# Edge counts by 90 groups of 14 destinations in pairs, in place of 60 windows of 21

## What is computed

```python
def rgat_conv(x, W, q, k, b, src, dst, etype, heads, out_ch, n_nodes):
    xr = jnp.einsum('nd,rdf->rnf', x, W)
    oi = xr[etype, dst]
    oj = xr[etype, src]
    qi = oi @ q
    kj = oj @ k
    alpha = jax.nn.leaky_relu(qi + kj, NEG_SLOPE)
    m = jax.ops.segment_max(alpha, dst, num_segments=n_nodes)
    e = jnp.exp(alpha - m[dst])
    z = jax.ops.segment_sum(e, dst, num_segments=n_nodes)
    a = e / (z[dst] + EPS)
    msg = (a[:, :, None] * oj.reshape(-1, heads, out_ch)).reshape(-1, heads * out_ch)
    out = jax.ops.segment_sum(msg, dst, num_segments=n_nodes)
    return out + b
```

## Time and profile before

| | |
|---|---|
| median of 3 runs | 1680.54 us (1675.92 to 1681.16) |
| profiled execution, first to last instruction | 1668.4 us |
| PE busy | 1571.1 us, 94% of the span |
| DVE busy | 1312.2 us, 79% |
| ACT busy | 808.3 us, 48% |
| POOL busy | 144.7 us, 9% |
| TensorE's clock, mean granted | 0.984 of full speed |

### The profile page before, as it was taken

The page is one execution under the profiler, slowest core; times in us unless marked ns, Lnnn a source line. Parts: engine busy times, 40 slices in busy tenths (PEclk is TensorE's granted clock), DMA queues, the critical chain, the costliest instruction groups (busy, mean ns, idle before and its releaser), DMA issues.

```text
span 1668.4 us, 34838 instructions
## 1 busy us (share of the span) xinstructions
PE 1571.1 (94%) x10783; PEld 1138.5 (68%) x10784; DVE 1312.2 (79%) x2631; ACT 808.3 (48%) x1072; POOL 144.7 (9%) x280
## 2 busy tenths in 40 slices
PE   5899988988999999999999999989999999999987
PEld 3566666766556666699999999976555555555544
DVE  8699869989479999288898998972774477777785
ACT  6331115552235654388888888962222233333342
POOL 3000010000100000000000000000000133333340
PEclk9999999999999999999999999989999999999999
DMA  6111125420456663540132133023765521101212
GB/s 208 37 60 62 62 59 171 156 81 29 134 183 219 200 200 120 175 136 31 62 94 62 31 116 118 12 92 93 211 202 190 191 96 56 37 20 56 76 51 93
DMA packets 129296, 178.56 MB, mean 107 GB/s; under 512 B 15510, under 2 KB 100607, under 8 KB 129203
## 3 DMA queue, kind: packets, MB, share of 16 engines
q1 hardware_dynamic: 129202, 177.38, 33.8%
HBM read 120.47 MB, written 56.88 MB: 106 GB/s over the span
## 4 chain that ended last, share of the span: by engine, by line
PE 70%; issue 16%; DVE 7%; ACT 2%; DMA 2%; DVEq 1%; POOL 1%; SPq 0%; POOLq 0%; ACTq 0%
PE ps L2210 23%; PE ps L2164 14%; PE ps L2270 7%; PE ps L2269 7%; PE ps L1983 5%; PE ps L2075 3%; PE ps L1970 2%; PE ps L1971 2%; PE ps L1972 2%; DVE oh_q L1466 1%; PE ps L2281 1%; PE ps L2147 1%; DVE oh_p L1467 1%; PE ps L2026 1%; DVE stat L1435 1%
## 5 line engine op out<-in xcount | busy, mean ns | idle before, releaser
L2210 PE MATMUL ps<-xrh,pf 128*128 (+1 forms) x2400 | 397.3, 328 | 4.8 <-DVE pf L1748 4.8
L2210 PEld LDWEIGHTS ps<-xrh,pf 128*128 128x128 f32 x2400 | 390.8, 190 | 11.2 <-issue 8.8
L2269 PE MATMUL ps<-x,ph 128*128 (+1 forms) x600 | 195.3, 325 | 12.1 <-POOL pl L989 12.0
L1970 PE MATMUL ps<-w_hi,xt_hi 128*128 128x384 f16 x600 | 196.9, 328 | 10.0 <-DVE ev L1794 3.2
L1748 DVE SCALAR_TENSOR_TENSOR pf<-vb,CT 128x1260 f32<-128x1260 f32 x118 | 172.8, 1467 | 32.5 <-PE ps L2210 32.5
L1971 PE MATMUL ps<-w_lo,xt_hi 128*128 128x384 f16 x600 | 196.9, 328 | 0.0
L2270 PE MATMUL ps<-x,ph 128*128 (+1 forms) x600 | 196.7, 328 | 0.0
L1972 PE MATMUL ps<-w_hi,xt_lo 128*128 128x384 f16 x600 | 196.6, 328 | 0.0
L1466 DVE TENSOR_SCALAR oh_q<-pat,codeT,neg_w 125x630 f16<-125x630 uint16 x420 | 185.2, 441 | 13.1 <-PE ps L1983 7.2
L1744 DVE SCALAR_TENSOR_TENSOR vb<-vb,tb 128x1260 f32<-128x1260 f32 x118 | 169.9, 1466 | 12.6 <-ACT vb L1220 11.7
L1656 DVE CUSTOM_DVE_ANT_0 tt_junk<-kbc,mb 126x1260 bf16<-126x1260 f32 x120 | 169.1, 1465 | 11.7 <-issue 11.7
(11 more groups left out here) (264 smaller groups left out, 2400.4 us busy)
## 6 DMA issues: line engine op xcount, KB each, us to landing
qbc<-tq_d SPq DMA_DIRECT2D x12, 1260.0 KB, 6.3
wst<-in_L_gnn_W SPq DMA_DIRECT2D x60, 192.0 KB, 3.2
xr_d<-ev SPq DMA_DIRECT2D x60, 192.0 KB, 2.0
x_d<-ev SPq DMA_DIRECT2D x60, 192.0 KB, 2.3
mb_d<-mb SPq DMA_DIRECT2D x30, 310.1 KB
mb<-mb_d SPq DMA_DIRECT2D x30, 310.1 KB
xrh<-xr_d SPq DMA_DIRECT2D x3, 2880.0 KB, 15.5
x<-x_d SPq DMA_DIRECT2D x2, 3840.0 KB, 18.3
```

The costliest lines, as they stand in the source:

```text
L1970: pe.matmul(ps[:, bank, 0:CW], a_hi, hi[:, k, :], start=(k == 0), stop=False)
L2210: mm = pe.matmul(out[b], pf[j][:, b * DB:b * DB + P], x, start=(first and b % 2 == 0), stop=False, skip_group_check=True)
L2269: pe.matmul(ps[:, bank, 0:CW], p, cols(off, off + CW), start=start, stop=False, skip_group_check=True)
```

## The change

- A window becomes a group of 14 destinations (WN = 14), 90 groups, which are worked on in 45 pairs. A tile of a group is `oh_q` of 420 columns and one matmul of 420 columns into one bank; the pair's two groups go to two neighbouring banks. ScalarE's copy and SyncE's store take a pair at a time (2 x 420 columns, 45 instead of 60).
- Each group has three fixed tiles (TF = 3) and a loop of single tiles, for which `oh_q` and `oh_p` have four rotating places (TR = 4) with semaphores counted tile by tile; place and tile are found in registers. From the edge lists of this input: 39 groups take one step of the loop and 51 take two, so 411 tiles, 9.13 for a pair (91 in W_K, 183 in W_V, 28 in W_S, 109 in W_Q).
- Each group has two table words (first tile with count; running total). PE and DVE thus read four words for each pair, where they read one for each window.
- The codes and slots of the fixed tiles are laid out ahead by POOL (`cw`, `sw`: a loop of 90 steps, each with one table read, an addition and a copy of 125 x 3), and VectorE waits for `cw_done`. The fixed `oh_q` is then made with one operand from memory instead of two.
- The pairs lie: 10 in W_K, 20 in W_V, 3 in W_S and 12 in W_Q (two for each query block, ahead of its fourth step and at its end). None lies in the attention. At the start of a query block PE reads eight words instead of three.
- CT comes back in units of three groups, `sel` and the selections for it are laid out for three groups (12 selections on POOL instead of 8), and three small operations on the table become one.

The diff, cut to its core:

```diff
-WN = 21
+WN = 14
 NWN = ND // WN
 KN = WN * R
 QN = NB * KN
-QH = QN // 2
-NTAB = 64
+NTAB = 96
...
-CT_EARLY = 14
-TF = 4
-TM = 3
-TG = TF + TM
+CT_EARLY = 7
+TF = 3
+TR = 4
+TG = 2 * TF + TR
 NTP = NT + 8
-MAXG = -(-(NT - TF) // TM)
+MAXG = NT - TF
+WU = WD // WN
+NWP = NWN // 2
...
+        cb = [place(f"cb{j}", [P, 2 * QN], U16, 185344 + 1696 * j) for j in range(2)]
+        cc_ = [place(f"cc{j}", [P, 2 * QN], U16, 141312 + 1696 * j) for j in range(2)]
+        cw = place("cw", [P, NWN * TF], F32, 173056)
+        sw = place("sw", [P, NWN * TF], F32, 174144)
+        tabrow = place("tabrow", [1, 2 * NTAB], I32, 175232)
...
-        def window(eng, w):
-
-            word = eng.value_load(tabrow[0:1, ds(w, 1)], min_val=0, max_val=(NWN * MAXG << 16) + (MAXG << 9) + NT)
+        def window(eng, s):
+
+            word = eng.value_load(tabrow[0:1, ds(2 * s, 1)], min_val=0, max_val=(MAXG << 9) + NT)
+            first = eng.value_load(tabrow[0:1, ds(2 * s + 1, 1)], min_val=0, max_val=NWN * MAXG)
             tile0 = eng.snap(word & 511, min_val=0, max_val=NT - 1)
-            count = eng.snap((word >> 9) & 127, min_val=1, max_val=MAXG)
-            first = eng.snap(word >> 16, min_val=0, max_val=NWN * MAXG)
+            count = eng.snap(word >> 9, min_val=1, max_val=MAXG)
             return tile0, count, first
 
+        def windows(eng, w):
+
+            return [window(eng, 2 * w + u) for u in range(2)]
+
         W_K, W_V, W_S, W_Q = 0, NB, 3 * NB, 3 * NB + 3
-        QW = 3
-        W_A = W_Q + QW * K6
-
-        def block_windows(i):
-
-            return range(W_A + i, min(W_A + i + 1, NWN))
-
-        assert W_A + NB >= NWN and WT_TILES == K6 * K6
+        QW = 2
+        assert W_Q + QW * K6 == NWP and WT_TILES == K6 * K6
...
-            sp.dma_start(ct_d[:, ds(w, 1), :].rearrange("p o n -> p (o n)"), stage[u][:, :]).then_inc(ct_out[u], 16)
+            sp.dma_start(ct_d[:, ds(2 * w, 2), :].rearrange("p o n -> p (o n)"), stage[u][:, :]).then_inc(ct_out[u], 16)
...
-            for i in range(NB):
-                for w in block_windows(i):
-                    store_window(sp, w, cc_, (w - W_Q) % 2)
...
-            pool.wait_ge(e_row, 7)
+            pool.wait_ge(tab_io, 32)
+            with pool.Fori(0, NWN) as s:
+                word = pool.value_load(tabrow[0:1, ds(2 * s, 1)], min_val=0, max_val=(MAXG << 9) + NT)
+                tf = nc.s_assert_within(pool.snap(word & 511, min_val=0, max_val=NT - 1), 0, NT - 1,
+                                        skip_runtime_bounds_check_because="the table holds first tiles of 0 to NT - 1")
+                pool.tensor_tensor(cw[0:ET, ds(TF * s, TF)], codeT[0:ET, ds(tf, TF)], neg_w[0:ET, ds(s, 1)].to_broadcast([ET, TF]), ALU.add)
+                pool.tensor_copy(sw[0:ET, ds(TF * s, TF)], sloT[0:ET, ds(tf, TF)]).then_inc(cw_done, 1)
...
-                act.activation(stage[u][:, :].rearrange("p (q n) -> p q n", q=2), ps[:, bank:bank + 2, 0:QH], ACT.Copy).then_inc(ct_ev, 1)
+                act.activation(stage[u][:, :].rearrange("p (q n) -> p q n", q=2), ps[:, bank:bank + 2, 0:QN], ACT.Copy).then_inc(ct_ev, 1)
...
-            for i in range(3):
+            for i in range(2):
                 dve.sem_inc(oh_free[i], 1)
-
-            def one_hot(u, codes, slots, k, w):
-
-                dve.tensor_scalar(oh_q[0:ET, u, :], pat[0:ET, :], codes[:, k:k + 1], neg_w[0:ET, ds(w, 1)], ALU.subtract, ALU.is_equal)
-                return dve.tensor_scalar(oh_p[0:ET, u, :], iota_l[0:ET, :], slots[:, k:k + 1], None, ALU.is_equal)
-
-            def one_hots(w, tile0, count, first):
-                tf = nc.s_assert_within(tile0, 0, NT - 1, skip_runtime_bounds_check_because="the table holds first tiles of 0 to NT - 1")
-                codes, slots = codeT[0:ET, ds(tf, TF)], sloT[0:ET, ds(tf, TF)]
-                for i in range(2):
-                    dve.wait_ge(oh_free[i], w + 1)
-                    for u in range(2 * i, 2 * i + 2):
-                        last = one_hot(u, codes, slots, u, w)
-                    last.then_inc(oh_rdy[i], 1)
-                with dve.Fori(0, count) as jj:
-                    n1 = dve.snap(first + jj + 1)
-                    t0 = dve.snap(nc.s_assert_within(tf + TM * jj + TF, TF, NTP - TM, skip_runtime_bounds_check_because="tile0 + TF + TM * count <= NTP for every window of the table"))
-                    more, more_slots = codeT[0:ET, ds(t0, TM)], sloT[0:ET, ds(t0, TM)]
-                    dve.wait_ge(oh_free[2], n1)
-                    for u in range(TM):
-                        last = one_hot(TF + u, more, more_slots, u, w)
-                    last.then_inc(oh_rdy[2], 1)
+            dve.sem_inc(oh_free[2], TR)
+
+            def one_hots(w, of_w):
+
+                for u in range(2):
+                    tile0, count, first = of_w[u]
+                    s = 2 * w + u
+                    dve.wait_ge(cw_done, s + 1)
+                    dve.wait_ge(oh_free[u], w + 1)
+                    for t in range(TF):
+                        dve.tensor_scalar(oh_q[0:ET, TF * u + t, :], pat[0:ET, :], cw[0:ET, ds(TF * s + t, 1)], None, ALU.is_equal)
+                        last = dve.tensor_scalar(oh_p[0:ET, TF * u + t, :], iota_l[0:ET, :], sw[0:ET, ds(TF * s + t, 1)], None, ALU.is_equal)
+                    last.then_inc(oh_rdy[u], 1)
+                    with dve.Fori(0, count) as jj:
+                        n1 = dve.snap(first + jj + 1)
+                        t0 = dve.snap(nc.s_assert_within(tile0 + jj + TF, TF, NTP - 1, skip_runtime_bounds_check_because="tile0 + TF + count <= NTP for every window of the table"))
+                        o = dve.snap((n1 & (TR - 1)) + 2 * TF, min_val=2 * TF, max_val=TG - 1)
+                        dve.wait_ge(oh_free[2], n1)
+                        dve.tensor_scalar(oh_q[0:ET, ds(o, 1), :].rearrange("p o n -> p (o n)"), pat[0:ET, :], codeT[0:ET, ds(t0, 1)],
+                                          neg_w[0:ET, ds(s, 1)], ALU.subtract, ALU.is_equal)
+                        dve.tensor_scalar(oh_p[0:ET, ds(o, 1), :].rearrange("p o n -> p (o n)"), iota_l[0:ET, :], sloT[0:ET, ds(t0, 1)],
+                                          None, ALU.is_equal).then_inc(oh_rdy[2], 1)
...
-                        of_w = window(dve, W_K + 2 * ii + j + 1)
+                        of_w = windows(dve, W_K + 2 * ii + j + 1)
                         k_sum(1, NB + 2 * ii + j, j)
-                        one_hots(W_K + 2 * ii + j + 1, *of_w)
+                        one_hots(W_K + 2 * ii + j + 1, of_w)
...
-                    if k in (1, 3, 4)[:QW - 1]:
-                        count_part(wa + (1, 3, 4).index(k) + 1)
+                    if k == 2:
+                        count_part(wa + 1)
...
-                count_part(wa + QW)
+                if more:
+                    count_part(wa + QW)
...
-                for w in block_windows(i):
-                    if w + 1 < NWN:
-                        count_part(w + 1)
...
-            def count_window(w, bank, count, first):
+            def count_windows(w, bank, of_w):
 
                 pe.wait_ge(ct_ev, w + 1)
-
-                def tile(u, start):
-                    for q in range(2):
-                        last = pe.matmul(ps[:, bank + q, 0:QH], oh_p[0:ET, u, :], oh_q[0:ET, u, q * QH:(q + 1) * QH],
-                                         start=start, stop=False, skip_group_check=True)
-                    return last
-
-                for i in range(2):
-                    pe.wait_ge(oh_rdy[i], w + 1)
-                    for u in range(2 * i, 2 * i + 2):
-                        last = tile(u, u == 0)
-                    last.then_inc(oh_free[i], 1)
-                with pe.Fori(0, count) as jj:
-                    n1 = pe.snap(first + jj + 1)
-                    pe.wait_ge(oh_rdy[2], n1)
-                    for u in range(TF, TG):
-                        last = tile(u, False)
-                    last.then_inc(oh_free[2], 1)
+                for u in range(2):
+                    _, count, first = of_w[u]
+                    pe.wait_ge(oh_rdy[u], w + 1)
+                    for t in range(TF):
+                        last = pe.matmul(ps[:, bank + u, 0:QN], oh_p[0:ET, TF * u + t, :], oh_q[0:ET, TF * u + t, :],
+                                         start=(t == 0), stop=False, skip_group_check=True)
+                    last.then_inc(oh_free[u], 1)
+                    with pe.Fori(0, count) as jj:
+                        n1 = pe.snap(first + jj + 1)
+                        o = pe.snap((n1 & (TR - 1)) + 2 * TF, min_val=2 * TF, max_val=TG - 1)
+                        pe.wait_ge(oh_rdy[2], n1)
+                        pe.matmul(ps[:, bank + u, 0:QN], oh_p[0:ET, ds(o, 1), :].rearrange("p o n -> p (o n)"),
+                                  oh_q[0:ET, ds(o, 1), :].rearrange("p o n -> p (o n)"),
+                                  start=False, stop=False, skip_group_check=True).then_inc(oh_free[2], 1)
...
```

(25 more changed lines are left out.)

101 lines of the change are left out of this document (47 added, 54 removed).

## The result

The changed kernel takes 1781.39 us (median of four runs, 1774.23 to 1783.8) against 1680.85 beside it: 1.0602 of the time before [1.0577, 1.0627], +100.5 us. The forecast was 1701.5, its range 1648 to 1748: the direction is right, the size far off.

The account below looks back on a forecast made before the run. Sequencer issue was taken to bound K and V: +34 there, -2.5 stalls, 0 S, 0 Q, -12 attention, +1.7 start, sum +21; span 1668.4 to 1689.4, plus 12.1 gives 1701.5 us, range 1648 to 1748.

Parts of the forecast that it names:

- issue bounds K and V: Key and value slots: sequencers' reads and steps, not arrays, set the pace; slot 4.87 to 6.0 us, +34; chance 0.45.
- together 6.0 us, if the vector operations' own issue costs nothing: VectorE's sequencer, each pair: four reads (1.8 us) plus some 47 register and branch steps (4.2).
- rivals A and B: K and V: A, arrays bound, 1644 to 1675, chance 0.33; B, cost and gain cancel, 1680.5 within 5, chance 0.12.
- C: K and V: issue worse on both engines, 7.3 us a slot, or POOL's loop late; 1753 us; chance 0.10.
- the spacing 0.62: VectorE, bias to next `oh_q`: 0.62 us with three register steps, no read; used to price a read at 0.33 to 0.59.
- S: Three windows among the sums: no net change, 0 us (-1 to +3.4).
- Q: Query blocks: TensorE's saving of 2.5 us a block against 2.3 for more reads at its head; 0 (-15 to +10).
- Attention: Attention stage: nine windows leave, at most -2.0 us each, limited by the lower clock; -12 (0 to -18).
- rival D: Attention: period stays at 6.0 us by a lower clock; adds 12, total 1713, counted inside the forecast's own range.
- Start: Before the first one-hot: three more table reads and POOL's work, less three small operations; +1.7 us (+0.5 to +3).
- Around the span: Outside the profiled span: 12.1 us (span against median of the runs), added to 1689.4 for the forecast time.
- the prediction's slot of 5.0: K and V slot with register loads at about 200 ns: 4.2 + 0.8 us, total below 1671.5; part of rival A's case.

Follow-up runs that it names:

- e7: Changed kernel with five fixed tiles, no loop, and four table reads a pair on TensorE alone, ahead of the product: slot 6.58 us, stage 235.1 against 187.1 without reads.
- e9: Changed kernel with four fixed tiles, a loop of exactly one step and no table reads on PE and DVE: 1661.9 us in one look.
- e15: The kernel of e9 again, in more runs: 1658.43 us, 0.988 of the kernel before [0.9852, 0.9908].

## Why the prediction was right and wrong

- **The mechanism was right**: issue bounds K and V, `V` waits for "issue", POOL's loop is not late (`oh_q` waits 2.3 us for `sw` in all), TensorE's matmul takes 0.177. "TensorE's list is as long" holds as well, 7.28 beside 7.27.
- **The step that failed** is "together 6.0 us, if the vector operations' own issue costs nothing". The slot is 7.88. Counted with 0.034 us of pause behind each row, VectorE's sequencer spends 2.76 on the reads (0.70 each), where 1.8 stood (0.45 each); 3.82 on 42 other rows (0.09 each), where 4.2 stood (47 at 0.09); 0.77 on issuing 19 operations (0.04 each, what a pause is longer for them), where nothing stood; and 0.52 in longer pauses, jumps back and some waits, where nothing stood. So the price of a step was right, that of a read was too low (0.70 lies above even its upper bound of 0.59), and two terms were put at nothing. K and V grew by 88.0 us, not 34, rivals A and B fall with it, and C's upper end of 7.3 a slot was too low as well.
- **Why a read came out at 0.45.** It rests on the spacing 0.62, taken for register steps alone. But VectorE's sequencer waited in it, from 148.40 to 148.76, for `oh_free`, which the fourth one-hot matmul of a window gives when it ends, at 148.72:

```profile
148.01 1.39 PE L1983 MATMUL ps<-oh_q,oh_p 125*128 125x315 f16 x9
...
L1473 DVEq ALU_OP  x1: 40/40/40, 148.4 to 148.4; - x1
...
L1466 DVEq ALU_OP  x1: 45/45/45, 148.8 to 148.8; - x1
```

  That pause is 0.36 us, where 0.05 is usual. With 0.31 for 0.62 the lower bound of a read is 0.86 - 0.31 + 0.09 = 0.64, not 0.33.
- **What the rows of the sequencer would have given**: in the trace before, a read takes 0.76 us with its pauses, another row 0.095 and the issue of an operation 0.04; VectorE's list is 3.58 a slot, where the prediction counted 2.6. Four reads, its 47 steps and 19 operations are by these prices 3.0 + 4.5 + 0.8 = 8.3 us (an estimate), against 7.88.
- **The clock in K and V** was priced at nothing. Granted 0.93 in place of 1.00, TensorE is 13.4 us longer busy there with fewer columns. In `e7` a wait ahead of a product was followed by such a stretch; what share of the 88.0 us the clock has was not isolated.
- **S**: 0 forecast, +11.8 measured; half is TensorE's reads, as `e7` shows. **Q**: 0 forecast (-15 to +10), +13.5. The argument had TensorE's eight reads late at the block's head; alone they cost nothing (124.5), while VectorE's reads (149.5) and its loops (148.6) each cost 20. So the argument had the wrong engine, and the loss lies outside its range. Why both together cost less (142.3, with 411 tiles in place of 450) is open.
- **Attention**: -12 forecast, -8.1 measured, and both of its cases occur. VectorE's `rdn`, one for each block:

```profile
498.72 0.23 DVE L1595 TENSOR_SCALAR rdn<-ps 128x6 f32<-128x6 f32 x2 [3.83 <-PE ps L2091]
...
505.04 0.24 DVE L1595 TENSOR_SCALAR rdn<-ps 128x6 f32<-128x6 f32 x2 [3.83 <-PE ps L2091]
...
521.26 0.23 DVE L1595 TENSOR_SCALAR rdn<-ps 128x6 f32<-128x6 f32 x2 [1.98 <-PE ps L2091]
...
525.73 0.23 DVE L1595 TENSOR_SCALAR rdn<-ps 128x6 f32<-128x6 f32 x2 [1.99 <-PE ps L2091]
```

  A block takes 6.3 us here, near the 6.4 of the prediction's case of the lower clock (rival D), and 4.46 at the end, near the 4.0 of the full clock. The granted clock is 0.54 in 498.70 to 511.40, 1.00 in 521.20 to 530.20, and 0.76 in the stage.
- **Start**: +1.7 forecast, none measured (the first one-hot matmul starts at 71.39, before at 71.40). **Around the span**: 1.7 us, not 12.1, for the profiled execution itself; the other 10.4 were the distance between executions of the kernel before, so 12.1 was no cost of launch and end. The rest of the layer, +8.2 us, lies between 1236.7 and 1245.5 us in these kernels, without a pattern, and differs by 5.0 between two executions of one kernel (`e9`, `e15`); it is not explained.

## What to carry to other kernels

Before replacing few long instructions by many short ones, sum each engine's instruction list, the sequencer's rows with the pauses between them, and compare it with the slot, not the arrays alone. Where a list already fills the slot, moving a read helps nothing; only a shorter list does. And before a price is taken from the spacing of two operations, look whether the sequencer waited between them.

## What the runs showed of the hardware

- A table word read into a register took 0.30 us on either engine, and 0.66 to 0.79 of VectorE's list in these kernels, with its address, check and assertion and the pauses between them. The Trainium skill, "Runtime: NRT & Kernel Launch", section Instruction fetch mechanics, gives some 200 ns for a register load, there from memory off the core, a kind that no run here has; the prediction's slot of 5.0 went by it, and a read of 0.66 or more leaves that slot no ground.
- Between two register rows the sequencer paused 0.034 us on VectorE and mostly 0.058 on TensorE; issuing an operation made VectorE's pause some 0.04 longer, a jump back to the head of a loop over tiles 0.1 longer.
- The instruction stream of an engine that is 62% busy (VectorE, 146.38 of 237 us) can still fill a stage: VectorE's list was 7.27 us of a slot of 7.88.
- A wait of 2.11 us ahead of a product of 18 matmuls cost another 1.5 through the clock, granted 0.65 in that stretch.
